# Third layer of a four-layer triangle network: 4 KB pieces by channel in DRAM, and an output stage over pairs of tiles

## The reference, cut to what matters

```python
def layer3(x):                          # x is already group-normalised
    h = layer_norm(x, norm_in_w, norm_in_b)            # over the 64 channels
    g = sigmoid(h @ g_in_w.T); p = h @ p_in_w.T        # 128 channels each
    a, b = split(g * p)                                # 64 channels each
    z = for every channel: a product of two 256 x 256 matrices (a with b)
    return sigmoid(h @ g_out_w.T) * (layer_norm(z, norm_out_w, norm_out_b) @ p_out_w.T)
x = x + layer3(_gn(x))
```

## Time and profile before

| | |
|---|---|
| median of three runs | 1610.25 us |
| the profiled execution | 1604.57 us |
| its span in the profile | 1602.6 us |
| TensorE matmul, busy | 1375.7 us, 86% |
| VectorE, busy | 1202.4 us, 75% |
| ScalarE, busy | 1011.7 us, 63% |
| GpSimd, busy | 438.4 us, 27% |
| read and written in HBM | 191.11 and 188.74 MB, 237 GB/s over the span |

### The profile page before, as it was taken

How to read it: one execution, slowest core, us unless ns; L and a number is a source line. 1 busy time by engine, 2 the same in 40 slices (tenths; PEclk the granted TensorE clock), 3 DMA queues, 4 the chain that set the end, 5 groups by cost and what they waited for, 6 DMA issues and landing times. The chain is left out here.

```text
span 1602.6 us, 25805 instructions
## 1 busy us (share of the span) xinstructions
PE 1375.7 (86%) x8728; PEld 750.3 (47%) x8733; DVE 1202.4 (75%) x1991; ACT 1011.7 (63%) x1641; POOL 438.4 (27%) x382
## 2 busy tenths in 40 slices
PE   5797699778695997799979999798889988995997
PEld 5535533223384442244449998122234437772443
DVE  5643687589699786778857777897778877998664
ACT  4675788744245887767746666555857765664555
POOL 5400099230000793320000000596320000001665
PEclk9798899899999998999989999898989999997999
DMA  9336410037886220379998886795068889995997
GB/s 352 118 144 243 177 53 14 1 101 211 256 278 251 80 93 0 131 257 333 334 318 304 301 302 232 279 381 194 37 243 334 333 321 363 419 418 213 399 406 300
DMA packets 151665, 381.56 MB, mean 238 GB/s; under 512 B 14704, under 2 KB 14960, under 8 KB 151408
## 3 DMA queue, kind: packets, MB, share of 16 engines
q1 hardware_dynamic: 139152, 356.63, 61.0%
q10 hardware_dynamic: 12384, 23.28, 3.9%
HBM read 191.11 MB, written 188.74 MB: 237 GB/s over the span
## 5 line engine op out<-in xcount | busy, mean ns | idle before, releaser
L1454 POOL TENSOR_TENSOR xT<-xT,work 128x512 f32<-128x512 f32 x192 | 240.7, 1270 | 637.4 <-DVE work L1499 635.4
L1131 PE MATMUL banks<-work 128*128 128x256 f32 x1408 | 335.4, 386 | 21.9 <-DVE work L1201 12.1
L1131 PEld LDWEIGHTS banks<-work 128*128 128x128 f32 x1408 | 261.8, 195 | 68.8 <-issue 17.9
L704 PE MATMUL banks<-work,w 64*64 64x512 f32 x2048 | 268.3, 612 | 15.1 <-DVE work L920 11.9
L920 DVE SCALAR_TENSOR_TENSOR work<-banks,bias,work 128x512 f32<-128x512 f32 x256 | 186.1, 747 | 59.8 <-PE banks L704 54.5
L820 ACT ACTIVATE work<-banks,bias 128x512 f32<-128x512 f32 x256 | 174.5, 686 | 63.5 <-PE banks L704 57.3
L1161 ACT COPY work<-banks 128x512 f32<-128x512 f32 x176 | 103.3, 587 | 153.9 <-PE banks L1131 151.0
L1499 DVE SCALAR_TENSOR_TENSOR work<-banks,bias,work 128x512 f32<-128x512 f32 x192 | 141.7, 747 | 39.3 <-ACT work L1429 19.6
L1643 POOL TENSOR_TENSOR xT<-xT,work 128x512 f32<-128x512 f32 x64 | 79.9, 1270 | 322.8 <-ACT work L1613 322.8
L1227 DVE TENSOR_TENSOR work<-work 128x512 f32<-128x512 f32 x176 | 121.0, 688 | 58.3 <-ACT work L1161 57.2
L704 PEld LDWEIGHTS banks<-work,w 64*64 64x64 f32 x2048 | 94.4, 134 | 150.0 <-DVE work L920 134.0
(11 more groups left out here) (165 smaller groups left out, 2067.0 us busy)
## 6 DMA issues: line engine op xcount, KB each, us to landing
hidden_rows<-work SPq DMA_DIRECT2D x128, 512.0 KB, 3.9
work<-hidden_rows SPq DMA_DIRECT2D x120, 512.0 KB, 6.8
products<-work SPq DMA_DIRECT2D x88, 512.0 KB, 3.8
work<-products SPq DMA_DIRECT2D x88, 512.0 KB, 4.8
work<-gate_rows SPq DMA_DIRECT2D x64, 512.0 KB, 5.5
work<-hidden SPq DMA_DIRECT2D x40, 512.0 KB, 5.8
work<-in_x SPq DMA_DIRECT2D x32, 512.0 KB, 4.6
gate_rows<-work SPq DMA_DIRECT2D x32, 512.0 KB, 2.8
```

The costliest lines, as they stand in the source:

```text
L704: mm = pe.matmul(out[side, :], w(name)[rows, side], h[rows, t % H, :], start=True, stop=True)
L1131: mm = pe.matmul(ZB[c % 2][:, r * N:r * N + N], a[:, kk, rows_of(r, c)], x[:, kk, :], start=(kk == 0), stop=(kk == 1))
L1454: pool.tensor_tensor(columns(t), columns(t), term[:, t % RING, :], ALU.add).then_inc(x_sb, 1)
```

## The change

Three things change, all in layer 3.

1. The row image of layer 3 gets its own DRAM tensor `hidden_pairs`, `(VP, 2, P, 2, T)`: pair, half, channel, tile of the pair, column. A projection store is now 128 pieces of 4 KB. Layer 4 keeps `hidden_rows`.
2. The products of layer 3 get the tensor `products2`, `(VP, 2, C, 2, T)`, likewise by channel. In the mix each channel is loaded and stored by itself: four loads of 256 KB per two channels where there were two of 512 KB, and two stores of 256 KB where there was one of 512 KB. In DRAM a piece is 4 KB, the two tiles of a pair; in SBUF these are two partitions of 2 KB. The output stage's load of z is one run of 512 KB, 4 KB per partition.
3. The output stage is a new function, `finish_pairs`. VectorE, ScalarE and GpSimd work on 1024 columns in one instruction. TensorE's matmuls stay at 512 columns (one bank). The two banks of `FAC` now belong to one pair, so the factors of pair p + 1 wait for the multiply of pair p (`at_least(pe, zn_sb, p)`).

```diff
+                      2: nc.dram_tensor("hidden_pairs", (VP, 2, P, 2, T), F32).ap(),
+                      3: nc.dram_tensor("hidden_rows", (2, VP, 2, P, T), F32).ap()}
...
+                         2: nc.dram_tensor("products2", (VP, 2, C, 2, T), F32).ap(),
...
+                    rows = (core.hid_d[2][u, half] if layer == 2 else
+                            core.hid_d[3][:, u, half].rearrange("w c x -> c w x"))
...
+        if by_channel:
+            return image[:, :, first, :, :].rearrange("v h w x -> (v h) w x")
...
+                    if by_channel:
+                        for c in (2 * g, 2 * g + 1):
+                            sp.dma_start(loaded(o, c), source(o, c, 1)).then_inc(landed[g % RING], 16)
+                        continue
...
+                if by_channel:
+                    for c in (2 * g, 2 * g + 1):
+                        sp.wait_ge(z_sb, c + 1)
+                        sp.dma_start(zdst[:, :, c, :, :].rearrange("v h w x -> (v h) w x"),
+                                     zs[:, c % (2 * OUT), :]).then_inc(stored[g % OUT], 16)
+                    return
...
+def finish_pairs(core, mask, sums, products_out):
...
+            for i in range(DUOS):
+                b = i % IN
+                at_least(sp, out_mm, 2 * (i - IN + 1))
+                sp.dma_start(z[:, b, :, :], core.products_of(2, i)).then_inc(landed[b], 16)
+                if i >= IN:
+                    sp.wait_ge(term_sb, i - IN + 1)
+                    load_gates(i)
...
+            def factors(p):
...
+                at_least(pe, zn_sb, p)
+                for t in (2 * p, 2 * p + 1):
...
+                    core.spread_factors(pe, 1, FAC[t % 2], spread[:, x, :], k).then_inc(fac_mm, 1)
...
+            factors(0)
+            for p in range(DUOS):
+                factors(p + 1)
+                pe.wait_ge(zn_sb, p + 1)
+                at_least(pe, term_sb, p - 1)
+                for t in (2 * p, 2 * p + 1):
+                    pe.matmul(OB[t % 4][:, :], w("pout"), z[:, p % IN, t % 2, :], start=True, stop=True).then_inc(out_mm, 1)
...
+                nc.scalar.activation(squares[:, p % 2, :, :], duo(p), ACT.Square, bias=core.shift,
+                                     accum_out=core.tile_sums[:, 1, p:p + 1]).then_inc(sq_sb, 1)
...
+                pool.tensor_tensor(duo(p), duo(p), term[:, p % 2, :, :], ALU.add).then_inc(x_sb, 1)
...
+                dve.wait_ge(landed[p % IN], 16 * (p // IN) + 16)
+                dve.wait_ge(fac_mm, 2 * p + 2)
+                dve.tensor_tensor(zt, core.banks[:, 0:2, :], zt, ALU.mult).then_inc(zn_sb, 1)
...
+            normed(0)
+            for p in range(DUOS):
+                normed(p + 1)
+                dve.wait_ge(gates_in[p % IN], 16 * (p // IN) + 16)
+                dve.wait_ge(out_mm, 2 * p + 2)
+                at_least(dve, x_sb, p - 1)
+                dve.scalar_tensor_tensor(out=term[:, p % 2, :, :], in0=core.banks[:, 4 + 2 * (p % 2):6 + 2 * (p % 2), :],
+                                         scalar=out_b, in1=gate[:, p % IN, :, :], op0=ALU.add, op1=ALU.mult,
+                                         accum_out=core.tile_sums[:, 0, p:p + 1]).then_inc(term_sb, 1)
+                if p == 1:
+                    first_shift()
...
-        finish(core, 2, 1, None, mask, sums, out)
+        finish_pairs(core, mask, sums, out)
```

More of the change, by code:

```diff
@@ L173, in __init__ @@
                       1: nc.dram_tensor("hidden1", (2, VP, 2, C, T), F32).ap(),
-                      2: nc.dram_tensor("hidden_rows", (2, VP, 2, P, T), F32).ap()}
-        self.hid_d[3] = self.hid_d[2]
-        self.products = {nq: nc.dram_tensor(f"products{nq}", (2, VP, 2, C // nq, T), F32).ap() for nq in (1, 2, 4)}
+                      2: nc.dram_tensor("hidden_pairs", (VP, 2, P, 2, T), F32).ap(),
+                      3: nc.dram_tensor("hidden_rows", (2, VP, 2, P, T), F32).ap()}
+        self.products = {0: nc.dram_tensor("products0", (2, VP, 2, C // 4, T), F32).ap(),
+                         1: nc.dram_tensor("products1", (2, VP, 2, C // 2, T), F32).ap(),
+                         2: nc.dram_tensor("products2", (VP, 2, C, 2, T), F32).ap(),
+                         3: nc.dram_tensor("products3", (2, VP, 2, C, T), F32).ap()}
         self.gate_d = nc.dram_tensor("gate_rows", (P, PITCH), F32).ap()
@@ L181, in two_banks, with products_of @@
         return self.banks[:, first:first + 2, :].rearrange("p n x -> p (n x)")
-    def products_of(self, nq, n):
-        return self.products[nq][:, nq * n:nq * n + nq].rearrange("w v h c x -> (v h c) w x")
+    def products_of(self, layer, n):
+        if layer == 2:
+            return self.products[2][n].rearrange("h c w x -> (h c) w x")
+        nq = {0: 4, 1: 2, 3: 1}[layer]
+        return self.products[layer][:, nq * n:nq * n + nq].rearrange("w v h c x -> (v h c) w x")
     def spread_factors(self, pe, nq, out, parts, k):
@@ L979, in store @@
                 for half in range(2):
-                    sp.dma_start(core.hid_d[layer][:, u, half].rearrange("w c x -> c w x"),
-                                 res[:, s, half + 1, :].rearrange("c (w x) -> c w x", w=2)).then_inc(stored[s], 16)
+                    rows = (core.hid_d[2][u, half] if layer == 2 else
+                            core.hid_d[3][:, u, half].rearrange("w c x -> c w x"))
+                    sp.dma_start(rows, res[:, s, half + 1, :].rearrange("c (w x) -> c w x", w=2)).then_inc(stored[s], 16)
             for u in range(PAIRS):
@@ L1014, in mix @@
     image = core.hid_d[layer]
-    zdst = core.products[C // cz]
+    zdst = core.products[layer]
+    by_channel = layer == 2
+    LOADS = 4 if by_channel else 2
     TB = [[bank[0], bank[1]], [bank[2], bank[3]]]
@@ L1057, in wait_loaded @@
                 g = c // 2
-                eng.wait_ge(landed[g % RING], 32 * (g // RING + (g % RING >= SINGLES // 2)))
+                eng.wait_ge(landed[g % RING], 16 * LOADS * (g // RING + (g % RING >= SINGLES // 2)))
         def wait_rows(eng):
@@ L1158, in out @@
                 if c % 2 == 0:
-                    at_least(act, stored[c // 2 % OUT], 16 * (c // 2 // OUT))
+                    at_least(act, stored[c // 2 % OUT], 8 * LOADS * (c // 2 // OUT))
                 at_least(act, s1_sb, c - 2 * OUT + 1)
@@ L1253, in _ @@
             summed(channels - 1)
-    return [(s, 16 * len(range(n, PAIRS, OUT))) for n, s in enumerate(stored)]
+    return [(s, 8 * LOADS * len(range(n, PAIRS, OUT))) for n, s in enumerate(stored)]
 class Roots:
@@ L1376, in _ @@
                 at_least(sp, out_mm, 2 * nq * (i - IN + 1))
-                sp.dma_start(z[:, b, :, :], core.products_of(nq, i)).then_inc(landed[b], 16)
+                sp.dma_start(z[:, b, :, :], core.products_of(layer, i)).then_inc(landed[b], 16)
                 if stored_gate and i >= IN:
@@ L1544, in load @@
                 at_least(sp, cen_mm, 2 * (u - IN) + 2)
-                sp.dma_start(z[:, u % IN, :, :], core.products_of(1, u)).then_inc(landed[u % IN], 16)
+                sp.dma_start(z[:, u % IN, :, :], core.products_of(3, u)).then_inc(landed[u % IN], 16)
             def load_gates(u):
```

65 lines of the change are left out of this document (added).

## The result

The changed kernel takes 1615.45 us (median of 19 runs, 1607.94 to 1627.85); the kernel before took 1608.54 in 19 runs beside them. The ratio is 1.0047 [1.0031, 1.0063]: slower by 7.6 us [5.0, 10.1] (the ratio on 1608.54; the medians differ by 6.9), where 1.8 was forecast. The time lies in the range of 1606.5 to 1619, but not by the forecast's mechanism: the range had been drawn wide enough to hold rival 2 (1616.5), and the loss has the form of that rival. For the forecast this is luck.

A forecast was written before the change was run, and what follows sets the result against it. TensorE was taken to hold the output stage, VectorE and DMA close behind. Projection -0.5, mix 0, steady output stage -1.0, its start and end +3.3 sum to +1.8 us on the median 1610.25: 1612.0, range 1606.5 to 1619.

The forecast's parts named there:

- rival 2: Output stage: the z load becomes the bound, 2.92 us a pair, +3.4 in place of -1.0, total 1616.5; chance 0.17.
- Projection and mix: Layer 3: projection 0 in its steady part and -0.5 us behind its last pair; mix 0, at 5.19 us a pair.
- the paragraph on the Trainium skill: Mix: the skill's page advises 1 MiB batches and puts 2.0 us fixed cost on each DMA, against halving transfers.
- The tail: From the projection's last stores to the first mix load: -0.5 us, bounds -1.5 and +0.3.
- Durations: Output stage: multiply 1.21 us, first output product to scalar_tensor_tensor 1.16 + 0.94 us, GpSimd's first add 2.5 us.
- TensorE's pair: Output stage: TensorE's work for a pair of tiles takes between 2.68 and 2.79 us.
- Rival 1: Output stage: the merged order gives TensorE more, 2.67 us a pair, -3.1 in place of -1.0, total 1610.0; chance 0.18.
- The steady output stage: Output stage, pairs 4 to 29: 2.75 us a pair against 2.79, together -1.0 us, bounds -3.1 and +3.4.
- L: Output stage: landing time of a z load; (L + 4.17)/3 us a pair, under 4.1 needed for 2.75.
- End: Output stage's end: GpSimd's add and ScalarE's square wait for whole 1024-column instructions; +3.3 us with the start included.
- Start: Output stage's start at 1.2 GHz: pair 4's output product at 1029.8 against tile 8's at 1028.10, +1.7 us.
- What bounds the kernel: Output stage before the change: held by TensorE, with VectorE and DMA close behind; VectorE hardly waits for DMA.

The follow-up runs named there:

- pairs alone: The pair-wise output stage added to the kernel before, with rows and products in DRAM as before (2 KB pieces): 1616.68 us, ratio 1.0067.

## Why the prediction was right or wrong, step by step

- *Projection and mix: right; the tail not shown.* The mix is 178.76 us against 178.92, at twice the packets. That also answers the paragraph on the Trainium skill: its page "DMA: Bandwidth & Descriptors" (section "Bandwidth") spoke against halving the transfers, and here, with TensorE busy for all of 135 us, that cost nothing. The 2.0 us of fixed cost stand there under the path of DMAs issued from GpSimd, those of the mix come from SyncE and ScalarE; the prediction doesn't say so, and nothing in its sum hangs on it. The tail, which answers to the earlier trace rows, is 4.73 us from the last stores to the first mix load, against 5.24. That looks like the forecast -0.5, but it is one profile: the second of after has 6.42 (before 5.18), and the nine profiles with the 4 KB stores go from 4.73 to 6.42, the four with the old ones from 5.03 to 6.42.

```profile
826.49 1.08 SPq L988 DMA_DIRECT2D hidden_pairs<-work  x2
...
831.22 1.49 SPq L1077 DMA_DIRECT2D work<-hidden_pairs  x2
```

- *Durations: right.* T takes 1224 ns (1.21), first O to S 2.08 us (1066.07 to 1068.15; forecast 1.16 + 0.94). GpSimd's add is 2350 ns (2.5).
- *TensorE's pair: forecast too high.* Forecast 2.68 to 2.79, found 2.53. Four F take 0.55 up to the first O where two took 0.34, and two O take 1.98 where each took 1.05: 0.13 and 0.12 less a pair, of which the forecast counted 0.11 on the side of O alone. Rival 1 came nearer on TensorE (2.67), and it bought nothing.
- *The steady output stage: this step failed.* It is "I take 2.75 a pair, for which L must stay under 4.1", with its reason that 4 KB pieces and three waiting engines "leave the queue some air". L was 5.3. The formula itself held: with L = 5.3 and the rest 3.9 (3.84 and the 0.05 from landing to T) in place of 4.17 it gives 3.07 a pair; 3.05 is what the z loads show (3.16 over the whole stretch below, with the stop at 1038.91). The rest was too large mostly by F, 0.82 with its gap against 0.61 from the end of T to O. That is rival 2, put at 0.17, beyond its own figure of 2.92 because it took L at its old 4.6. From O of pair 4 (1032.72) to O of pair 31 (1117.96) went 85.24 us, before 75.31 (1028.10 to 1103.41): +9.9 against -1.0.
- *Why L was mis-sized.* I took the rate of 4 KB pieces from layer 4's mix. That stretch has loads that land after 8.1 us and stores after 7.3: landings, weighted by count, over 1.25 us per transfer make 6.2 transfers in flight. The output stage had (4.6 + 5.1)/2.79 = 3.5 of them before. So its rate could not be read off that stretch, and the piece doesn't set it: pairs alone with 2 KB pieces and after with 4 KB differ by 7 GB/s (340, 333). (The number in flight is worked out from landing and pace, so it doesn't say which of them is the cause.) The lead of a z load, which the prediction itself had at 4.9 us before, became 3 x 2.79 - 3.84 = 4.5 at the old pace and 3 x 2.53 - 3.84 = 3.75 at TensorE's own; both are under every median landing of the stage in the kernels that load the gates. The prediction named the limit of 4.1 beside a median of 4.6 and chose the value on the wrong side of its own rows; with 4.6 it would have had rival 2's time as its forecast. Why the landing also rose from 4.6 to 5.3 with as many in flight stays open; the layout doesn't do it, since it rises with 2 KB pieces too (5.2). Part of the rise may be scatter: the second profile of before has 4.9, and the tile-wise kernel in the new layout 5.3 and 4.8.
- *End: right. Start: too dear.* O of pair 4 comes 25.82 us into the stage against 25.32: +0.5 (forecast +1.7). Of the 1.2 too much, 0.6 stands already at the first S (16.65 us into the stage against 17.2; the cold F and O took less) and most of the rest in the warm F, 0.55 each against 0.8. The end is +1.7 (forecast +1.6): from O of pair 31 to the next stage 7.44 us against 5.70. These two rows hold the end:

```profile
1119.18 4.64 POOL L1615 TENSOR_TENSOR xT<-xT,work 128x1024 f32<-128x1024 f32 x2 [1.23 <-DVE work L1645]
...
1123.85 1.15 ACT L1608 ACTIVATE work<-xT,fold 128x1024 f32<-128x1024 f32 x1 [1.06 <-POOL xT L1615]
```

- *What bounds the kernel: only partly right.* "The stage is held by TensorE, with VectorE and DMA close behind" fits the busy time, but four buffers in the old, tile-wise stage gained 4.2 us. With a lead of 4.9 us and landings of 4.6 to 4.9 in the median before stood at the edge of waiting, and its profile showed an execution that was faster than the runs.

Sum by stage, in the first profile: -0.5 + 0 + 0.5 + 9.9 + 1.7 = +11.6, of which the -0.5 is scatter as far as the other profiles tell. The second pair of profiles has a stage longer by 8.0, and the runs say 7.6 [5.0, 10.1] for the whole.

## What to carry to other kernels

When a stage's unit of work is doubled, write down for each load its lead: buffers times the new pace, less the time from the first use of the data to the issue of the next load into the same buffer, and compare it with the landing times that the trace has, at the faster pace that is hoped for. A buffer more is only of use if no other load in the same queue waits for something later ahead of it; here, with pairs, z alone gained little (1.0034 against 1.0047, the intervals overlap) and z and gates together, with a second set of FAC banks, 0.9952. And take a transfer rate from a stretch with as many transfers in flight, not from one with the same piece size.

## What the runs showed of the hardware

- *Rate against transfers in flight* (512 KB each, rate and landings of the stage): 333 GB/s at (5.3 + 5.3)/3.05 = 3.5, 399 at (6.9 + 6.5)/2.56 = 5.2, and 418 in layer 4's mix at 6.2. Before had 374 to 381 at 3.5, so the number is not all. At 5.2 the pace was TensorE's own; whether more in flight would give more there wasn't run.
- *Landing under load.* The same z load takes 3.3 us at 201 GB/s, 4.6 to 5.4 at 333 to 381 with three buffers for z, 6.1 to 6.2 at 346 to 353 with four, 6.9 to 7.2 at 389 to 399 with four for the gates too, all medians. A buffer more makes the landing longer, not only the lead.
- *A packet ends where a partition's piece ends.* The mix moved the same bytes in 22216 packets where it had 11066, at 301 and 300 GB/s: DMA share 0.92 against 0.82, no change in time.

```profile
q1 hardware_dynamic: 22216, 40.44, 91.8%
```

- *The order of matmul groups.* F F F F O O (four F, two products) takes 2.53 us; in the order F F O, F F O it took 2.79 with the same columns, both at a granted clock of 1.00.
- *GpSimd's add* grows by less than its columns: 2350 ns for 1024, 1271 for 512 (page of after), so merging saves 0.19 us a pair, and gives it back at the end of the stage, where ScalarE must wait for the whole.
